# Waits by counts in the first stage, contiguous key scales, and fewer GpSimd operations for values and shifts

## The reference, cut to what matters

```python
kv = (cond @ Wkv + bkv).reshape(1, -1, 2, H, hd)      # 16 heads of 16
k, v = kv[:, :, 0], kv[:, :, 1]
q = _fq_sym(q * scale, axis=-1)   # scale: the largest |.| of each token's head / 127
k = _fq_sym(k, axis=-1)           # the same, for each key's head
v = _fq_sym(v, axis=2)            # one scale for a column, over all 24,000 keys
attn = jnp.einsum('bhqd,bhkd->bhqk', q, k)
attn = softmax(attn, axis=-1)
attn = _fq_unsigned(attn, axis=-1)                    # 255 levels, the row's largest is 255
out = jnp.einsum('bhqk,bhkd->bhqd', attn, v)
...
out @ Wp + bp
```

## Time and profile before

| what | us |
|---|---|
| median of 3 runs (lowest to highest) | 4506.83 (4506.46 to 4507.93) |
| the profiled execution | 4505.41 |
| its span, first to last instruction | 4503.7 |
| PE busy in it | 4293.8 (95%) |
| DVE busy | 4020.6 (89%) |
| POOL busy | 3679.2 (82%) |
| ACT busy | 3525.6 (78%) |

### The profile page before, as it was taken

How to read it: one execution, slowest core, us unless ns; L and a number is a source line. 1 busy time by engine, 2 the same in 40 slices (tenths; PEclk the granted TensorE clock), 3 DMA queues, 4 the chain that set the end, 5 groups by cost and what they waited for, 6 DMA issues and landing times. The chain is left out here.

```text
span 4503.7 us, 134862 instructions
## 1 busy us (share of the span) xinstructions
PE 4293.8 (95%) x54175; PEld 1769.0 (39%) x54175; DVE 4020.6 (89%) x7371; ACT 3525.6 (78%) x3643; POOL 3679.2 (82%) x4026
## 2 busy tenths in 40 slices
PE   7888888999999999999999999999999999888999
PEld 5666663333333333333333333333333333224655
DVE  6888888999999999999999999999999999884333
ACT  3555557899999999999999999999999999882111
POOL 5777777999999999999999999999999999872000
PEclk9999998999999999999999999999999999999999
DMA  3555542111111111111111111111111111442010
GB/s 103 162 165 170 168 151 68 36 36 33 37 35 33 37 35 34 36 34 34 37 33 36 35 34 36 33 36 35 34 36 37 31 38 32 158 147 94 0 39 9
DMA packets 222678, 267.79 MB, mean 59 GB/s; under 512 B 34366, under 2 KB 202809, under 8 KB 221289
## 3 DMA queue, kind: packets, MB, share of 16 engines
q1 hardware_dynamic: 167529, 203.57, 16.1%
q10 hardware_dynamic: 54528, 55.60, 3.9%
HBM read 174.57 MB, written 82.97 MB: 57 GB/s over the span
## 5 line engine op out<-in xcount | busy, mean ns | idle before, releaser
L1580 ACT ACTIVATE e_home<-ps_scores,sk 125x896 f32<-125x896 f32 x3072 | 3076.7, 1009 | 276.8 <-PE ps_scores L1318 68.2
L1614 DVE TENSOR_REDUCE unit_max<-ps_maxima 128x1 f32<-128x428 f32 (+2 forms) x5760 | 3068.7, 607 | 28.1 <-PE ps_maxima L1346 20.1
L1801 POOL TENSOR_SCALAR r<-e_home 125x896 f32<-125x896 f32 x2976 | 2759.0, 956 | 187.6 <-POOLq L104 94.4
L1374 PE MATMUL ps_maxima<-e_home,unit 125*17 125x224 f32 x24576 | 1691.7, 352 | 8.2 <-DVE r L1648 7.2
L1318 PE MATMUL ps_scores<-q,k_home 54*128 54x448 bf16 x5760 | 1585.2, 355 | 3.1 <-PEq L1493 2.9
L1346 PE MATMUL ps_maxima<-k_home,q 48*128 48x428 bf16 (+2 forms) x5760 | 1574.9, 351 | 2.1
L1366 PE MATMUL ps_maxima<-r,vt 125*16 125x224 f16 x12288 | 850.7, 267 | 32.6 <-DVE r L1648 21.0
L1318 PEld LDWEIGHTS ps_scores<-q,k_home 54*128 54x128 bf16 x5760 | 323.5, 95 | 1060.7 <-issue 1045.6
L1366 PEld LDWEIGHTS ps_maxima<-r,vt 125*16 125x16 f16 x12288 | 294.4, 85 | 1060.0 <-issue 831.2
L1374 PEld LDWEIGHTS ps_maxima<-e_home,unit 125*17 125x17 f32 x24576 | 616.8, 95 | 13.8 <-DVE r L1648 7.5
L1346 PEld LDWEIGHTS ps_maxima<-k_home,q 48*128 48x128 bf16 x5760 | 376.6, 93 | 56.4 <-DVE unit_max L1614 44.6
(11 more groups left out here) (272 smaller groups left out, 2738.2 us busy)
## 6 DMA issues: line engine op xcount, KB each, us to landing
k_rows<-krows ACTq DMA_DIRECT2D x48, 1000.0 KB, 6.9
k_home<-k_rows SPq DMA_DIRECT2D x408, 93.8 KB
k_home<-k_rows SPq DMA_DIRECT2D x120, 281.2 KB
e_home<-in_ctxT SPq DMA_DIRECT2D x48, 500.0 KB, 5.4
vr<-v_raw SPq DMA_DIRECT2D x128, 187.5 KB
cb<-in_ctxT SPq DMA_DIRECT2D x16, 1500.0 KB, 6.1
v_raw<-e_home SPq DMA_DIRECT2D x12, 1000.0 KB
v_raw<-vb SPq DMA_DIRECT2D x12, 1000.0 KB
```

The costliest lines, as they stand in the source:

```text
L1374: made = pe.matmul(psav[c:c + WIDE, lo:hi], unit[:, :], e[(i + s) % SLOTS][0:KT, g, lo:hi], start=head_first and part == 0, stop=False, sk ...
L1580: act.activation(e[i % SLOTS][0:KT, :, :], score_banks(i)[0:KT, :, :], ACT.Exp, scale=sk[u][:, i:i + 1]).then_inc(e_wrote[h % 2], 1)
L1614: top = dve.tensor_reduce(maxima[y][:, b, slot:slot + 1], ps[:, 0:hi - lo], axis=AX.X, op=ALU.max)
L1801: pool.tensor_scalar(r[i % SLOTS][:, :, :], e[i % SLOTS][0:KT, :, :], 1.0, WHOLE_WORD, ALU.mult, ALU.add)\
```

## The change

In the first stage every `wait_ge(sem, 1).then_inc(sem, -1)` between engines becomes a wait for a count that only goes up (`Passed`, moved out of the second stage), on all four engines; at the start of a round counts of 96 and more are taken down by 96. The waits of `dve_done` and `pool_done` stay as they are, and so do those for DMAs.

The scales of the keys go into `tile_scale`, two buffers of one chunk in [tile, head] order, which lie in `av` and `wp`; ACT copies each full buffer in [head, tile] order to `k_scale`, after its high part of the chunk's last generation, eight times in all.

The addition of ln 255 leaves the shift: it is a bias column of the exponential (`levels`). The sign is put into `sq` once. The six bf16 columns of the shift are written in another order (high, middle, high, middle, high, low) by copies with a broadcast input, so that four operations follow the multiplication on DVE and on POOL; the rows of the keys' scales are stored in the matching order. On POOL the halves of the values are multiplied without a wait behind each, then rounded in two operations over all 384 elements, at steps 7 and 10. PE waits for one signal of them instead of two. One small buffer (`q0_in`) moves.

```diff
+SETTLED = 96
...
+    levels = sbuf(key_st, "levels", [KT, 1])
...
     def head_max(h1, columns=NCH * NPIECE):
...
-        dve_done(dve.tensor_scalar(shift[:, :], shift[:, :], -1.0, LOG255, ALU.mult, ALU.add))
+    def shift_copies(n):
+        return shift[:, :].rearrange("p (b o) -> p b o", o=1).to_broadcast([QB, NQB, n])
+    HIGH, MID, LOW = slice(0, SROWS, 2), slice(1, SROWS - 1, 2), SROWS - 1
+    T_ROWS = ((0, 1, 5), (2, 3), (4,))
     def high_part():
-        dve_done(dve.tensor_copy(shift_parts[:, :, 0], shift[:, :]))
+        dve_done(dve.tensor_copy(shift_parts[:, :, HIGH], shift_copies(3)))
         dve_done(dve.tensor_tensor(shift[:, :], shift[:, :], shift_parts[:, :, 0], ALU.subtract))
     def other_parts():
-        dve_done(dve.tensor_copy(shift_parts[:, :, 1], shift[:, :]))
-        dve_done(dve.tensor_tensor(shift_parts[:, :, 2], shift[:, :], shift_parts[:, :, 1], ALU.subtract))
-        dve.tensor_copy(shift_parts[:, :, 3:5], shift_parts[:, :, 0:2])
-        dve.tensor_copy(shift_parts[:, :, 5], shift_parts[:, :, 0]).then_inc(shift_ready, 1)
+        dve_done(dve.tensor_copy(shift_parts[:, :, MID], shift_copies(2)))
+        dve.tensor_tensor(shift_parts[:, :, LOW], shift[:, :], shift_parts[:, :, 1], ALU.subtract)\
+           .then_inc(shift_ready, 1)
     def scaled_values(h, half):
...
-        pool_done(pool.tensor_tensor(part, part, ...))
+        pool.tensor_tensor(part, part, ...).then_inc(v_scaled, 1)
-    def whole_values(x, half):
-        tiles = slice(half * VTILES, (half + 1) * VTILES)
-        pool_done(pool.tensor_scalar(x[:, tiles, :], vr[:, tiles, :], ROUND, ROUND, ALU.add, ALU.subtract))
+    def raised_values():
+        pool.wait_ge(v_scaled, 2).then_inc(v_scaled, -2)
+        pool.tensor_scalar(vr[:, :, :], vr[:, :, :], 1.0, ROUND, ALU.mult, ALU.add).then_inc(v_raised, 1)
+    def whole_values(x):
+        pool.wait_ge(v_raised, 1).then_inc(v_raised, -1)
+        pool_done(pool.tensor_scalar(x[:, :, :], vr[:, :, :], 1.0, -ROUND, ALU.mult, ALU.add))
         pool.sem_inc(vt_ready, 1)
-        if half == 1:
-            pool.sem_inc(vr_free, 1)
+        pool.sem_inc(vr_free, 1)
+    class Passed:
+        def __init__(self, engine, sem):
+            self.engine, self.sem, self.seen = engine, sem, 0
+        def next(self, n=1):
+            self.seen += n
+            return self.seen
+        def settle(self, block=QUAD):
+            while self.seen >= block:
+                self.engine.sem_inc(self.sem, -block)
+                self.seen -= block
...
+        tile_scale = [x.rearrange("p (t h) -> p t h", h=HEADS) for x in (av[0:KT, 0:CT * HEADS], wp[...])]
...
-        def tiles_of(x, n, lo, count):
-            return x[:, :, n * GEN + lo:n * GEN + lo + count].rearrange("p h t -> p t h")
+        def scales_in_turn(n, lo, count):
+            j, at = divmod(n * GEN + lo, CT)
+            return tile_scale[j % 2][:, at:at + count, :]
...
-                    pe.wait_ge(k_free, 1).then_inc(k_free, -1)
+                    pe.wait_ge(k_free, k_free_seen.next())
...
-                dve.wait_ge(scale_step, 1).then_inc(scale_step, -1)
+                dve.wait_ge(scale_step, scale_step_seen.next())
...
+            dve.wait_ge(sq_landed, 16).then_inc(sq_landed, -16)
+            dve_done(dve.tensor_scalar(sq[:, :, :], sq[:, :, :], -1.0, None, ALU.mult))
             for n in range(NGEN - 4, NGEN):
...
-                pool.wait_ge(kr_ready, 1).then_inc(kr_ready, -1)
-                pool.tensor_tensor(q4, ints(n), per_head(tiles_of(k_scale, n, 0, GEN), GEN), ALU.mult)\
+                pool.wait_ge(kr_ready, kr_ready_seen.next())
+                pool.tensor_tensor(q4, ints(n), per_head(scales_in_turn(n, 0, GEN), GEN), ALU.mult)\
...
+            def turn_tile_scales(j):
+                kept = tile_scale[j % 2].rearrange("p t h -> p h t")
+                act.activation(k_scale[:, :, j * CT:(j + 1) * CT], kept, ACT.Copy)\
+                   .then_inc(scales_kept, 1)
...
                 if in_stage(n - 1):
                     high_part(n - 1)
+                if n > 0 and n % (CT // GEN) == 0 and in_stage(n - 1):
+                    turn_tile_scales(n * GEN // CT - 1)
...
-    SCALED, WHOLE, CHAINED = (1, 4), (SLOTS - 1, SLOTS + 2), 13
+    SCALED, RAISED, WHOLE, CHAINED = (1, 4), 7, 10, 13
...
-                    pe.wait_ge(vt_ready, 2).then_inc(vt_ready, -2)
+                    pe.wait_ge(vt_ready, 1).then_inc(vt_ready, -1)
...
-                               scale=sk[u][:, i:i + 1]).then_inc(e_wrote[h % 2], 1)
+                               bias=levels[:, 0:1], scale=sk[u][:, i:i + 1]).then_inc(e_wrote[h % 2], 1)
...
-                pool_done(pool.tensor_scalar(shift[:, :], shift[:, :], -1.0, LOG255, ALU.mult, ALU.add))
-                for part in range(2):
-                    pool_done(pool.tensor_copy(shift_parts[:, :, part], shift[:, :]))
-                    rest = shift[:, :] if part == 0 else shift_parts[:, :, 2]
-                    pool_done(pool.tensor_tensor(rest, shift[:, :], shift_parts[:, :, part], ALU.subtract))
-                pool_done(pool.tensor_copy(shift_parts[:, :, 3:5], shift_parts[:, :, 0:2]))
-                pool.tensor_copy(shift_parts[:, :, 5], shift_parts[:, :, 0]).then_inc(shift_ready, 1)
+                pool_done(pool.tensor_copy(shift_parts[:, :, HIGH], shift_copies(3)))
+                pool_done(pool.tensor_tensor(shift[:, :], shift[:, :], shift_parts[:, :, 0], ALU.subtract))
+                pool_done(pool.tensor_copy(shift_parts[:, :, MID], shift_copies(2)))
+                pool.tensor_tensor(shift_parts[:, :, LOW], shift[:, :], shift_parts[:, :, 1], ALU.subtract)\
+                    .then_inc(shift_ready, 1)
```

More of the change, by code:

```diff
@@ L55 @@
 WHOLE_WORD = 8388608.0
+LOG255 = math.log(255.0)
 HALF_UNIT = 2.0 ** -24
@@ L619, in pe_program @@
             for n in range(NGEN):
+                for passed in (k_free_seen, v_free_seen, low_ready_seen, turn_free_seen, rows_kept_seen, s_free_seen):
+                    passed.settle(SETTLED)
                 piece = pieces(n - 4)
@@ L654, in pe_program @@
             shift_rows()
-            pe.wait_ge(s_free, 4).then_inc(s_free, -4)
-            pe.wait_ge(k_free, 2).then_inc(k_free, -2)
-            pe.wait_ge(turn_free, 2).then_inc(turn_free, -2)
-        def dve_program():
+            pe.wait_ge(s_free, s_free_seen.next(4))
+            pe.wait_ge(k_free, k_free_seen.next(2))
+            pe.wait_ge(turn_free, turn_free_seen.next(2))
+            for passed in (k_free_seen, v_free_seen, low_ready_seen, turn_free_seen, rows_kept_seen, s_free_seen):
+                passed.clear()
+        def dve_program():
+            s_full_seen = Passed(dve, s_full)
+            k_full_seen = Passed(dve, k_full)
+            scale_step_seen = Passed(dve, scale_step)
+            x_done_seen = Passed(dve, x_done)
+            top_done_seen = Passed(dve, top_done)
+            parts_free_seen = Passed(dve, parts_free)
+            v_biased_seen = Passed(dve, v_biased)
             def keys_of(m):
@@ L763, in dve_program @@
                 n, p = divmod(m, 2)
+                for passed in (s_full_seen, k_full_seen, scale_step_seen, x_done_seen, top_done_seen, parts_free_seen, v_biased_seen):
+                    passed.settle(SETTLED)
                 if m == 4:
@@ L782, in dve_program @@
                     value_top(n - 1, p)
-                scale = tiles_of(k_scale, n, 2 * p, 2)
+                scale = scales_in_turn(n, 2 * p, 2)
                 scale_wait()
@@ L821, in dve_program @@
             dve.sem_inc(q2_ready, 1)
-            dve.wait_ge(parts_free, 4).then_inc(parts_free, -4)
+            dve.wait_ge(parts_free, parts_free_seen.next(4))
+            for passed in (s_full_seen, k_full_seen, scale_step_seen, x_done_seen, top_done_seen, parts_free_seen, v_biased_seen):
+                passed.clear()
         def pool_program():
+            kr_ready_seen = Passed(pool, kr_ready)
+            high_ready_seen = Passed(pool, high_ready)
+            mid_ready_seen = Passed(pool, mid_ready)
+            v_kept_seen = Passed(pool, v_kept)
             def scale_parts(n):
@@ L836, in add_bias @@
             def add_bias(n):
-                pool.wait_ge(v_kept, 1).then_inc(v_kept, -1)
+                pool.wait_ge(v_kept, v_kept_seen.next())
                 lo = n % 2 * GEN
@@ L857, in pool_program @@
             for n in range(NGEN):
+                for passed in (kr_ready_seen, high_ready_seen, mid_ready_seen, v_kept_seen):
+                    passed.settle(SETTLED)
                 q4, r4 = by_head(kq[n % 2]), by_head(rest[n % 2])
@@ L954, in copy_scales @@
                 act.sem_inc(turn_free, 1)
-                for row in ((0, 1, 2), (3, 4), (5,))[r]:
+                for row in T_ROWS[r]:
                     act.dma_start(t_rows[row, batch].rearrange("(q b) k -> q b k", b=TB), t_rows_sb[:, r, :, :])\
@@ L1000, in act_program @@
             for n in range(NGEN + 4):
```

(14 more changed lines are left out.)

115 lines of the change are left out of this document (60 added, 55 removed).

## The result

| | before | changed |
|---|---|---|
| median of 4 runs, us | 4507.26 (4506.46 to 4507.93) | 4482.8 (4480.31 to 4484.18) |
| profiled execution / its span | 4505.4 / 4503.7 | 4480.3 / 4477.8 |
| ratio to before | | 0.9946, interval 0.9935 to 0.9958 |
| PE / DVE / POOL / ACT busy | 4293.8 / 4020.6 / 3679.2 / 3525.6 | 4293.5 / 4015.9 / 3598.3 / 3738.0 |

What follows compares the result with a forecast made beforehand. First stage bound by handoffs between PE, DVE and POOL; then PE and DVE at 100%, POOL 96%. 17 + 1.5 + 0.7 + 11.6 - 1 = 29.8 us gained: 4477 us as a median, range 4449 to 4497.

Steps and rivals of the forecast that it cites:

- Waits by counts: First stage: about 0.1 us saved per handoff where the waiter was first; 17 us, plus 1.5 in the drain.
- three handoffs of 0.10: POOL and DVE loop: POOL for kept values, DVE for the bias, POOL for whole keys; 0.30 us a generation, 14.1 us.
- rival A: Waits cost nothing, only operations do, or the path's handoffs are others: 4495.5 us, chance 0.12.
- Contiguous scales: First stage, DVE's scale and POOL's multiplication by the keys' scales: strided access is not slower, gain 0.
- Rival C: Contiguous scales speed POOL's key scaling on the loop by a third, 31 us more: 4446 us, chance 0.06.
- Turned copies: ACT's eight copies into k_scale, near 0.5 us each, mostly covered by idle ACT: 1 us lost.
- Shift on DVE and drain: End of the first stage: a scalar operation and two copies on DVE go, all on the path: 0.7 us gained.
- PE's stalls for POOL: Heads' last chunks: 15 waits for roundings vanish, 11.6 us; POOL gains 0.9 by values, 1.0 by shift, against 0.84 waited.
- Value operations: POOL, each chunk: two operations of 384 elements, multiply and add, take 0.5 us each.
- I take 0: Second stage: level as bias column of ACT's exponential costs 0; ACT, busy 94%, covers up to 0.06 us a step.
- in ordinary chunks nobody waits for it: Second stage: POOL's 0.9 us gain a chunk from the value operations brings 0 in ordinary chunks.
- signs I had named: Generation under 13.3 us, bias gap 0.18, k_scaled gap under 0.1, no 0.8 PE gap, value operations together under 1.5.

Runs made afterwards that it cites:

- e1: Kernel before with only the first stage's waits by counts on all four engines (and the sign in sq): 4489.5 us, ratio 0.9963.
- e7: Kernel before with the first stage's waits by counts on POOL and DVE alone: 4495.3 us, ratio 0.9976.
- e8: Kernel before with the first stage's waits by counts on PE and ACT alone: 4504.2 us, ratio 0.9994.
- e3: Changed kernel with the keys' scales written and read strided in k_scale again, without ACT's copies: 4486.6 us, ratio 0.9956 to the kernel before.
- e9: Kernel before with a bias column of zeros added to each exponential, the level still in the shift: 4507.6 us, ratio 1.0006.
- e2: Changed kernel with the level added in the shift again and no bias column: 4474.3 us, ratio 0.9932 to the kernel before.
- e5: Kernel before with the new value operations on POOL alone: 4495.2 us, ratio 0.9977.
- e6: Kernel before with the new order of the shift's columns alone, the level still added: 4495.4 us, ratio 0.9976.
- e4: Kernel before with the level moved from the shift into the exponential's bias column: 4502.1 us, ratio 0.999.
- e11: Changed kernel measured a second time, nothing altered: 4481.7 us, ratio 0.9946 to the kernel before.
- e12: Second measurement of the changed kernel with the level in the shift and no bias column: 4479.1 us, ratio 0.9938 to the kernel before.

## Why the prediction was nearly right, point by point

**Waits by counts, 17 in the stage and 1.5 in the drain: right in sum.** e1 measures 16.5 us for the launch, 15.1 in the loop. The three handoffs of 0.10 that I counted are visible, and e7 puts 11.9 us on POOL and DVE (I had 14.1 there), with 2.8 for PE and ACT, which I had not priced apart. The drain's 1.5 was wrong: e1, e7 and e8 have drains 0.5 to 0.9 longer. The rule of the Trainium skill that I made rival A (VectorE: DVE Perf Modes, The DRAIN you can't avoid) is about one engine with a signal behind each operation. What costs here is the wait that takes its semaphore down, and for that e1 decides against the rival.

**Contiguous scales, 0: too low.** 2.012 to 1.928 us, 3.3 to 5.5 us of the loop (e3). My comparison with L897 was no measure: its inputs are an f32 and a bf16 one as L892's are, but they are not plain, since the bf16 part lies in runs of 16 elements out of 48. The strided scales step 192 floats, 768 bytes, and not the 960 that I wrote. Rival C's third, after the Trainium skill's 50% for inner steps over 8 bytes (GPSIMD Engine Reference, Performance pitfalls for Q7 kernels), is not seen: 4%, with scales reread for 16 elements.

**Turned copies, 1: 0.** They take 0.85 us, not 0.5, and ACT's slack hides them.

**Shift on DVE and drain, 0.7: not shown.** The drain did get 2.0 us shorter, but e9's does as well, 36.3, with the old shift, and e2's with the new shift is 38.3. It seems to hang in part on the last stores of key rows: ACT issues one at 679.96 before and can reuse its buffer at 691.39, 11.4 us later; in e9 it is 679.04 to 689.15, 10.1 us. That isn't all of it: in e3 it is 11.1 us (663.70 to 674.83) with a drain of 36.7. All five kernels with the bias column have drains of 36.1 to 37.0, the others 37.6 to 39.2. What the column has to do with the drain stays open.

**PE's stalls for POOL, 11.6: right.** Heads 0 to 14 lost 12.5, and the line is gone. e5 and e6 add that one of the two edits is enough; the forecast had them as a sum, 0.9 and 1.0 against a need of 0.84, and either covers it.

**Value operations, 0.5 each: right**, 0.51 for f32 and for f16.

**The step that failed is the bias column, "I take 0", with the cover read from the stage around 2000 us.** ACT's 94% there left 0.06 us a step, the column takes 0.09, and even so the 15 heads hardly grew (2.3 us in e9). The stage where cover was missing was another, the last head, whose steps were 0.89 us by ACT's own pace; I had no row from it. The same holds for the values: "in ordinary chunks nobody waits for it" is true of 15 heads and not of the last, where POOL and DVE share the roundings. Together these cost 8.1 us. The Trainium skill had the price of the column: ScalarE: Activation LUTs, What ACT_TABLE_LOAD costs, states some 93 ns for each per-partition operand of an ACTIVATE. The trace agrees, 1099 against 1009 ns. By the page's figure, as an estimate, the 192 steps of the last head would be at most 17.9 us longer. The last heads traced are 1.6 (e9) and 5.6 us longer (e4) with the old value operations, and 3.6 to 8.2 longer beside the new ones (e11 against e12, changed against e2).

Of the signs I had named, four came: generations under 13.3 us (13.10), the bias add's gap of 0.18, no gap of PE for POOL at the products in the heads' last chunks, two value operations under 1.5 us (1.02). The gap before k_scaled, which I wanted under 0.1, is 0.12.

The sum again: -1.1 (start), -15.1 (counts), -3.5 (scales), -2.0 (drain), -12.5 (stalls), +8.1 (last head) is -26.1, and the spans differ by 25.9. That the total came so near is in part luck: the unforeseen 8.1 is half made up by gains that I had at nothing or lower (the scales, the start, the stalls), and the drain's 2.0 came although neither term that I had for it is shown.

## What to carry to other kernels

Where engines take turns, count the handoffs on the loop whose waiter was there first: here a wait that also takes its semaphore down cost about 0.1 us at each, and a count that only rises removed it. Cover must be read in every stage that an instruction runs in, above all in the first and last pass of a loop, where a neighbour's work is missing and another engine sets the pace. Of two edits that each lift the same stall, only one pays, and the other can still cost elsewhere: here old value operations with all the rest (e10) are 7 us faster than the whole change.

## What the runs showed of the hardware that was not expected

- A per-partition bias column makes an ACTIVATE of 896 elements 0.09 us longer, with zeros in it (e9, 1101 ns against 1009) as with ln 255 (1099).
- Slower exponentials shortened stalls: step 14 of the last head's chunks went from 1.64 to 0.98 us in e9, and 2.2 us of added instruction time a chunk became 0.6.
- The same kernel (e2, e12) had runs in two groups, around 4473 and 4479, and the two traced ones differ in how many steps PE spent at the 1.2 GHz level, though the waits of 1.79 us in front of them stand in both.
